# A feed-forward block on one core: down projection in rounded halves over three engines, selection keys in PSUM, transposes between products

## The reference, cut to what matters

```python
inter = xf @ c1_w.T @ c2_w.T                       # rank 16, 1792 columns
blk = inter.reshape(B * T, n_blocks, SPARSITY)     # 56 blocks of 32
idx = jnp.argmax(blk, axis=-1) + jnp.arange(0, INTER, SPARSITY)
h = jax.nn.relu(jnp.einsum('bkm,bm->bk', w1[idx], xf))
out = jnp.einsum('bk,bkm->bm', h, w2t[idx])
```

## Time and profile before

| | us |
|---|---|
| median of 3 runs (lowest to highest) | 625.63 (625.03 to 625.82) |
| the profiled execution's own time | 625.32 |
| its span in the trace | 623.3 |

### The profile page before, as it was taken

One profiled execution on the slowest core, in us unless ns is written; L12 is line 12 of the kernel. 1 busy time (PEld: TensorE's weight loads), 2 busy tenths in 40 slices (PEclk: granted clock), 3 DMA queues, 4 the chain that ended last, 5 costly groups with the idle time before them and its releaser, 6 DMA issues.

```text
span 623.3 us, 10995 instructions
## 1 busy us (share of the span) xinstructions
PE 611.2 (98%) x3900; PEld 523.7 (84%) x3900; DVE 437.0 (70%) x882; ACT 332.6 (53%) x613; POOL 222.8 (36%) x181
## 2 busy tenths in 40 slices
PE   8999999999999999999999989999999999999997
PEld 8888888799898999899988989997979779787573
DVE  4533137678888888888886768799794774858773
ACT  2513115668676867677776635755544554447110
POOL 0000002269778877887786712224012021000000
PEclk9999999999999999999999999999999999999999
DMA  7500011878887788788778929485765767697500
GB/s 263 226 0 31 5 38 40 214 191 213 215 213 198 202 213 214 200 209 212 178 178 227 340 98 302 153 323 201 270 252 218 282 221 261 252 366 312 195 1 17
DMA packets 29693, 120.67 MB, mean 194 GB/s; under 512 B 7712, under 2 KB 8224, under 8 KB 22096
## 3 DMA queue, kind: packets, MB, share of 16 engines
q1 hardware_dynamic: 28912, 118.96, 61.1%
q10 hardware_dynamic: 576, 1.05, 0.6%
q0 software_dynamic: 160, 0.07, 0.1%
HBM read 86.30 MB, written 0.26 MB: 139 GB/s over the span
## 4 chain that ended last, share of the span: by engine, by line
PE 81%; POOL 6%; DVE 6%; issue 4%; ACT 3%; DVEq 0%; ACTq 0%; POOLq 0%
PE ps L1767 20%; PE ps L1466 10%; PE ps L1467 10%; PE ps L1468 10%; PE ps L1807 9%; PE ps L1567 4%; POOL pt_lo L542 3%; PE ps L1796 2%; PE ps L1643 2%; PE ps L1918 2%; DVE prob_far L1116 2%; PE ps L1510 2%; PE ps L1527 2%; POOL v_lo L542 2%; PE ps L1881 2%
## 5 line engine op out<-in xcount | busy, mean ns | idle before, releaser
L1767 PEld LDWEIGHTS ps<-norm_t,ring 128*128 128x128 f32 x1152 | 131.6, 192 | 4.9 <-issue 4.1
L1767 PE MATMUL ps<-norm_t,ring 128*128 128x128 f32 x1152 | 133.2, 276 | 0.0
L542 POOL TENSOR_TENSOR pt_lo<-far_t,pt_hi 128x512 fp32r<-128x512 f32 (+1 forms) x94 | 111.8, 1216 | 55.1 <-ACT pt_hi L658 54.6
L732 ACT ACTIVATE prob_far<-prob_far,neg_max 128x1024 f32<-128x1024 f32 (+2 forms) x96 | 85.5, 892 | 55.2 <-DVE neg_max L1120 55.2
L1116 DVE TENSOR_SCALAR_CACHE_REDUCE prob_far<-ps 128x256 f32<-128x256 f32 (+2 forms) x96 | 86.8, 906 | 31.9 <-PE ps L1468 31.5
L1297 DVE SCALAR_TENSOR_TENSOR acc<-raw,cw,acc 128x127 f32<-128x127 f32 (+2 forms) x240 | 77.0, 397 | 19.5 <-ACT acc L909 18.9
L1140 DVE STREAM_TRANSPOSE prob_far<-prob_far 128x2176 f32<-128x2176 f32 x30 | 73.1, 2436 | 0.8 <-ACT prob_far L732 0.2
L1466 PE MATMUL ps<-pt_hi,v_hi 128*128 128x256 f32 x208 | 61.2, 294 | 2.7 <-POOL pt_lo L542 2.3
L1466 PE MATMUL ps<-k_hi,q_hi 128*128 128x512 f32 (+2 forms) x160 | 61.4, 384 | 1.4 <-ACT v_all L658 0.7
L1468 PE MATMUL ps<-pt_lo,v_hi 128*128 128x256 f32 x208 | 58.8, 283 | 0.0
L1467 PE MATMUL ps<-pt_hi,v_lo 128*128 128x256 f32 x208 | 58.7, 282 | 0.0
(11 more groups left out here) (228 smaller groups left out, 1144.1 us busy)
## 6 DMA issues: line engine op xcount, KB each, us to landing
ring<-w_in_dram SPq DMA_DIRECT2D x36, 1024.0 KB, 4.9
far_t<-prob_far SPq DMA_DIRECT2D x240, 136.0 KB, 2.6
ring<-w_out_dram SPq DMA_DIRECT2D x16, 1024.0 KB, 4.8
ring<-wq_dram SPq DMA_DIRECT2D x16, 512.0 KB, 4.1
ring<-wo_dram SPq DMA_DIRECT2D x16, 512.0 KB, 3.6
w_sb<-w_dram SPq DMA_DIRECT2D x4, 896.0 KB, 9.1
ring<-ctx_t_dram SPq DMA_DIRECT2D x3, 1024.0 KB, 5.1
ring<-w_dram SPq DMA_DIRECT2D x3, 1024.0 KB, 8.8
```

The costliest lines, as they stand in the source:

```text
L542: sub = lambda dst, a, hi: pool.tensor_tensor(dst, a, hi, ALU.subtract)
L732: nc.scalar.activation(tile, tile, ACT.Exp, bias=neg_max[:, b, h:h + 1], accum_out=part_sum[:, b, h, i:i + 1]).then_inc(exp_ok, 1)
L1767: ins = mm(ps[:, bank, t * T:t * T + T], w[:, t, c, :], norm_t[:, c, :], start=(c == 0), stop=(c == NC - 1))
```

## The change

The down projection is done as three rounded products per tile. The work of splitting goes to three engines:
- ScalarE: `w2_high(c)` copies chunk c of `w2` from `ring` into the new `w2_hi` (rounded); chunk 0 ahead of the wait for the square root of L999, chunk 1 behind it, chunks 2 and 3 behind the copy `r1_st`. The copies out of PSUM now write `hsel_hi` in the rounded type.
- GpSimd: `ring_lo = ring - w2_hi`, in place, in pieces of 1024 columns (two, two, two and one), each chunk behind its copy.
- VectorE: `selected_low(i)` subtracts `hsel_hi` from the transposed quarter in PSUM. Number 0 comes behind the first step of quarter 2's selection, number 1 behind the fourth, 2 and 3 behind all of the selection.

The keys of the selection stay in PSUM bank i: the two equality and product steps write there, in place, only the last mask goes to SBUF (`key[i % 2]`). `key` and `hsel` are two buffers of 512 columns each in place of one of 1792. `turn_over(2)` now comes behind tile 5 of the down projection and `turn_over(3)` behind tile 9. `w2_hi` is laid over buffers of the state-space block, which are moved for it; the final sum is written into `normed` in place of `final`. The number of transfers and their sizes are the same.

```diff
@@ -246,13 +246,13 @@
                 bc = sbuf(st4, "bc", [P, 16, T])
                 gm = sbuf(st4, "gm", [P, GROUPS, T])
                 with ExitStack() as st5:
-                    key_flat = sbuf(st5, "key", [P, FF])
-                    hsel = sbuf(st5, "hsel", [P, FF])
-                    hsel_t = sbuf(st5, "hsel_t", [P, NFT, T])
+                    key = [sbuf(st5, f"key{b}", [P, BANK]) for b in range(2)]
+                    hsel = [sbuf(st5, f"hsel{b}", [P, BANK]) for b in range(2)]
+                    hsel_hi = sbuf(st5, "hsel_hi", [P, NFT, T], F32R)
+                    hsel_lo = sbuf(st5, "hsel_lo", [P, NFT, T], F32R)
                     rank = sbuf(st5, "rank", [P, BLK])
                     norm_hi = sbuf(st5, "norm_hi", [P, NC, T], F32R)
                     norm_lo = sbuf(st5, "norm_lo", [P, NC, T], F32R)
-                    final = sbuf(st5, "final", [P, DM])
                 raw = [sbuf(st4, f"raw{b}", [P, 4, T]) for b in range(2)]
                 acc = [sbuf(st4, f"acc{b}", [P, 4, T]) for b in range(2)]
                 xc = [sbuf(st4, "xc0", [P, TPG, T])]
@@ -260,20 +260,21 @@
                 decay = [sbuf(st4, "decay0", [P, HPG, T])]
                 xc.append(sbuf(st4, "xc1", [P, TPG, T]))
                 sg.append(sbuf(st4, "sg1", [P, TPG, T]))
+                with ExitStack() as same_place:
+                    w2_hi = sbuf(same_place, "w2_hi", [P, NFT * DM], F32R)
+                at_pair.append(sbuf(st4, "at_pair1", [P, HPG, HALF_T], F32R))
+                at_hi.append(sbuf(st4, "at_hi1", [P, HPG, HALF_T], F32R))
+                at_lo.append(sbuf(st4, "at_lo1", [P, HPG, HALF_T], F32R))
                 decay.append(sbuf(st4, "decay1", [P, HPG, T]))
                 xdt = sbuf(st4, "xdt", [P, HPG, 64])
                 yv = sbuf(st4, "yv", [P, TPG, T])
                 ysq = sbuf(st4, "ysq", [P, TPG, T])
                 sq_tok = sbuf(st4, "sq_tok", [P, 2, T])
                 ug = [sbuf(st4, f"ug{b}", [P, TPG, T]) for b in range(2)]
-                at_pair.append(sbuf(st4, "at_pair1", [P, HPG, HALF_T], F32R))
-                at_hi.append(sbuf(st4, "at_hi1", [P, HPG, HALF_T], F32R))
-                at_lo.append(sbuf(st4, "at_lo1", [P, HPG, HALF_T], F32R))
 
                 with ExitStack() as same_place:
                     w1_lo = sbuf(same_place, "w1_lo", [P, NC, FF], F32R)
                 w1_sb = sbuf(st4, "w1_sb", [P, NC, FF])
-            key = key_flat[:].rearrange("p (n j) -> p n j", j=BLK)
 
         last_wo_hi = k_hi[:, 0:2 * DM].rearrange("p (h n) -> p h n", h=2)
         last_wo_lo = k_lo[:, 0:2 * DM].rearrange("p (h n) -> p h n", h=2)
@@ -321,6 +322,7 @@
                                                sem("nl_ok"))
         ug_ok, var_s = sem("ug_ok"), sem("var_s")
         f_mask = sem("f_mask")
+        w2h_ok, w2l_ok, htl_ok = sem("w2h_ok"), sem("w2l_ok"), sem("htl_ok")
         pair_const, a_pair_in = sem("pair_const"), sem("a_pair_in")
         stored = sem("stored")
 
@@ -527,7 +529,7 @@
                 s, before = stream(FFN0 + c)
                 load(s, w2[c] if c < 3 else w2_tail[0], before)
             sp.wait_ge(final_ok, 1)
-            sp.dma_start(out, final[:]).then_inc(stored, 16)
+            sp.dma_start(out, normed[:]).then_inc(stored, 16)
             sp.wait_ge(stored, 16)
 
 
@@ -651,6 +653,15 @@
                     sub(c2_st[64:64 + RANK, :], c2_sb[64:64 + RANK, :],
                         c2_st[64:64 + RANK, :].bitcast(F32)).then_inc(c2l_ok, 1)
                     pool.wait_ge(c2l_ok, 1)
+
+            for c in range(4):
+                slot, cols = stream(FFN0 + c)[0], min(SLOT, NFT * DM - c * SLOT)
+                pool.wait_ge(w2h_ok, c + 1)
+                for at in range(0, cols, SLOT // 2):
+                    part = slice(at, at + SLOT // 2)
+                    i = sub(ring_lo[slot][:, part], ring[slot][:, part],
+                            w2_hi[:, c * SLOT + at:c * SLOT + at + SLOT // 2].bitcast(F32))
+                i.then_inc(w2l_ok, 1)
 
 
         @block.scalar
@@ -995,8 +1006,19 @@
             mamba_step(6, 0, True)
 
             squares(GROUPS - 1)
+            def w2_high(c):
+
+
+                slot, before = stream(FFN0 + c)
+                cols = min(SLOT, NFT * DM - c * SLOT)
+                act.wait_ge(landed[slot], 16 * (before + 1))
+                act.wait_ge(*((seg_ps, 2 * GROUPS), (y_ps, GROUPS), (y_ps, GROUPS), (ug_ok, 2 * GROUPS))[c])
+                copy(w2_hi[:, c * SLOT:c * SLOT + cols], ring[slot][:, 0:cols]).then_inc(w2h_ok, 1)
+
+            w2_high(0)
             act.wait_ge(var_s, 4)
             nc.scalar.activation(rstd[:, 1:2], rstd[:, 0:1], ACT.Sqrt).then_inc(var_s, 1)
+            w2_high(1)
 
 
             norm_sqrt(2)
@@ -1004,10 +1026,12 @@
             copy(norm_hi[:], ps[:, 7, :].rearrange("p (c t) -> p c t", c=NC)).then_inc(nh_ok, 1)
             act.wait_ge(r1_ps, 1)
             copy(r1_st[:], ps[0:STACK, 6, 0:T]).then_inc(r1h_ok, 1)
+            w2_high(2)
+            w2_high(3)
             for i in range(4):
                 w = min(4, NFT - 4 * i)
                 act.wait_ge(ht_ps, i + 1)
-                copy(hsel_t[:, 4 * i:4 * i + w, :],
+                copy(hsel_hi[:, 4 * i:4 * i + w, :],
                      ps[:, i, 0:w * T].rearrange("p (c t) -> p c t", t=T)).then_inc(ht_ok, 1)
 
 
@@ -1425,30 +1449,45 @@
             sub(r1_st[32:32 + RANK, :], ps[32:32 + RANK, 6, 0:T],
                 r1_st[32:32 + RANK, :].bitcast(F32)).then_inc(r1l_ok, 1)
             dve.wait_ge(pool_const, 8)
+            def selected_low(i):
+
+                w = min(4, NFT - 4 * i)
+                dve.wait_ge(ht_ok, i + 1)
+                sub(hsel_lo[:, 4 * i:4 * i + w, :], ps[:, i, 0:w * T].rearrange("p (c t) -> p c t", t=T),
+                    hsel_hi[:, 4 * i:4 * i + w, :].bitcast(F32)).then_inc(htl_ok, 1)
+
             for i in range(4):
                 lo, hi = i * BANK, min(i * BANK + BANK, FF)
                 n0, n = lo // BLK, (hi - lo) // BLK
-                blocks = ps[:, i, 0:hi - lo].rearrange("p (n j) -> p n j", j=BLK)
-                k, top, first = key[:, n0:n0 + n, :], bmax[:, n0:n0 + n], kmax[:, n0:n0 + n]
+                k = ps[:, i, 0:hi - lo].rearrange("p (n j) -> p n j", j=BLK)
+                top, first = bmax[:, n0:n0 + n], kmax[:, n0:n0 + n]
                 dve.wait_ge(inter_ps, i + 1)
-                nc.vector.tensor_reduce(top, blocks, AX_X, ALU.max).then_inc(f_mask, 1)
+                nc.vector.tensor_reduce(top, k, AX_X, ALU.max).then_inc(f_mask, 1)
+                if i == 2:
+                    selected_low(0)
                 dve.wait_ge(f_mask, 5 * i + 1)
-                nc.vector.tensor_tensor(k, blocks, top.unsqueeze(2).to_broadcast([P, n, BLK]),
+                nc.vector.tensor_tensor(k, k, top.unsqueeze(2).to_broadcast([P, n, BLK]),
                                         ALU.is_equal).then_inc(f_mask, 1)
                 dve.wait_ge(f_mask, 5 * i + 2)
                 nc.vector.tensor_tensor(k, k, rank[:].unsqueeze(1).to_broadcast([P, n, BLK]),
                                         ALU.mult).then_inc(f_mask, 1)
                 dve.wait_ge(f_mask, 5 * i + 3)
                 nc.vector.tensor_reduce(first, k, AX_X, ALU.max).then_inc(f_mask, 1)
+                if i == 2:
+                    selected_low(1)
                 dve.wait_ge(f_mask, 5 * i + 4)
-                nc.vector.tensor_tensor(k, k, first.unsqueeze(2).to_broadcast([P, n, BLK]),
+                chosen = key[i % 2][:, 0:hi - lo]
+                nc.vector.tensor_tensor(chosen.rearrange("p (n j) -> p n j", j=BLK), k,
+                                        first.unsqueeze(2).to_broadcast([P, n, BLK]),
                                         ALU.is_equal).then_inc(f_mask, 1)
                 dve.wait_ge(f_mask, 5 * i + 5)
                 dve.wait_ge(h_ps, i + 1)
-                nc.vector.scalar_tensor_tensor(hsel[:, lo:hi], ps[:, 4 + i, 0:hi - lo], 0.0, key_flat[:, lo:hi],
+                nc.vector.scalar_tensor_tensor(hsel[i % 2][:, 0:hi - lo], ps[:, 4 + i, 0:hi - lo], 0.0, chosen,
                                                ALU.max, ALU.mult).then_inc(hsel_ok, 1)
+            selected_low(2)
+            selected_low(3)
             dve.wait_ge(ffn_ps, 1)
-            nc.vector.tensor_tensor(final[:], res[:], ps[:, 4, :], ALU.add).then_inc(final_ok, 1)
+            nc.vector.tensor_tensor(normed[:], res[:], ps[:, 4, :], ALU.add).then_inc(final_ok, 1)
 
 
         @block.tensor
@@ -1888,7 +1927,8 @@
 
                 pe.wait_ge(hsel_ok, i + 1)
                 for t in range(4 * i, min(4 * i + 4, NFT)):
-                    ins = nc.tensor.transpose(ps[:, i, (t % 4) * T:(t % 4 + 1) * T], hsel[:, t * T:t * T + T], ident[:])
+                    ins = nc.tensor.transpose(ps[:, i, (t % 4) * T:(t % 4 + 1) * T],
+                                              hsel[i % 2][:, (t % 4) * T:(t % 4 + 1) * T], ident[:])
                 ins.then_inc(ht_ps, 1)
 
```

(26 more changed lines are left out.)

## The result

| | before | after |
|---|---|---|
| median of 5 runs, us (lowest to highest) | 625.03 (624.72 to 625.82) | 627.54 (626.85 to 628.72) |
| ratio to before, 95% interval | | 1.0039 (1.0028 to 1.0049) |
| profiled execution: its time; its span | 625.32; 623.3 | 627.54; 625.8 |

The kernel is 2.5 us slower, where 1.3 was forecast; the time lies inside the range of 624.2 to 627.9.

The account below looks back on a forecast made before the run. TensorE was taken to bound the kernel, except VectorE's chain at the layer norm. From the profiled 625.32, stalls add 2.62 and the tail gives 1.3: 626.6, or 626.9 us against the median; range 624.2 to 627.9.

Parts of the forecast that it names:

- The products: Down projection on TensorE: 42 rounded passes of 0.2325 us replace 28 of 0.430, 2.28 us less if TensorE never waits.
- Who feeds them: Down projection: TensorE waits for VectorE's low half only ahead of tile 8, 0.95 us; the tail gains 1.3 us.
- Keys in PSUM: VectorE's selection steps: PSUM operands taken to cost 0, at most 0.06 us more for each of 16 steps.
- ScalarE's copies: The w2_high copies, 1.92 us per full chunk, fit into ScalarE's idle time and cost nothing.
- The first stall: w1_split(3), ahead of the layer norm, waits for GpSimd's piece 2: +0.52 us on the chain, 1.1 us being slack.
- The second stall: normed in the layer norm waits for GpSimd's piece 4: 2.1 us of the +2.6 on the chain.
- Rival B: Layer norm: normed isn't held by GpSimd, only the 0.52 us remains, 624.9 us; chance 0.24.
- the last rival, F: TensorE's clock falls after the longer pause at the layer norm: some 3 us more, 630; chance 0.05.
- A: Likeliest case: GpSimd holds both w1_split(3) and normed around the layer norm, 626.9 us; chance 0.52.
- rival D: Selection steps that write PSUM are dearer, +0.06 us on 16 steps: 627.9 us, or 625.9 without norm stall; 0.09 beside A.

Follow-up runs that it names:

- e6: e1 with selected_low(2) moved ahead of the last two steps of quarter 3's selection: 623.04 us against 625.28 before the change.
- e7: e1 with the selection's keys written to SBUF again instead of PSUM: 629.36 us against 625.28 before the change.
- e1: The change with all of GpSimd's pieces started only behind the copy norm_hi, after the layer norm: 623.48 us against 625.17 before the change.
- e2: The change with only the first chunk's two GpSimd pieces early, the other five behind norm_hi: 623.97 us against 625.17 before the change.
- e3: The change with the layer norm's sum written to PSUM and normed reading it there: 625.35 us against 625.17 before; once more, 624.97 against 625.14.
- e5: The change with GpSimd's pieces halved to 512 columns, 14 instead of 7: 624.41 us against 625.28 before the change.
- e4: The change with 22 instead of 12 warming products on TensorE: 626.07 us against 625.17 before the change.
- e12: The change with the edits of e2 and e3 and 16 instead of 12 warming products: 624.29 us against 625.40 before the change.

## Why the prediction was right, and where it was off

- **The products**: 0.2325 us per pass was forecast; chain and timeline of after show 0.23. In e6, where no stall is left in the norm, selection to store takes 21.76 us against 23.66, 1.90 less, with 0.35 of delay left at tile 8 (its chain has 0.11 us of issue there and 0.47 us for a pass instead of 0.23). 1.90 + 0.35 = 2.25, against 2.28.
- **Who feeds them**: right by place and size. One wait, ahead of tile 8, 0.83 us against 0.95, none elsewhere. The restart adds a little (starts of 616.76 and 617.98 lie 1.22 apart instead of 0.23, and the next one 0.31), so the tail gave 1.10 and not 1.3.
- **Keys in PSUM**: I took 0 and it was 0.01: 0.70 where a step writes PSUM. The bound of 0.06 a step wasn't needed. That they cost nothing is the small part of it; e7 shows what they save, of which my prediction said nothing, as it costed only their price.
- **ScalarE's copies**: 1.90 us for a full chunk, under cover, as forecast; the square root still waits for VectorE (1.4 us).
- **The first stall**: +0.52 forecast, +0.48 measured, 0.45 by e1 and e2. The mechanism, read from the earlier trace rows, held within 0.05 us: `w1_split(3)` took 3.65 us against the 3.70 of the sum.
- **The second stall**: +2.1 forecast, +1.98 measured on the step itself. Piece 4 was 0.09 us ahead of `normed`, where I had 0.05. Rival B was refuted on the point that it hung on; e3 and e5 confirm the reason.
- **What failed** is the last rival, F, by its weight: "A small chance", with 0.05. It came with A, in all five executions. TensorE's pause of 2.83 us was followed by 1.45 us of loss (e4: 1.47). Its price was off as well, "some 3 us": the lower level held from about 597.3 to 600.7, not for all of the products behind the pause. Without the clock the tail would have grown by 1.32 us, as in e4, and the forecast of +1.3 was made for that. I had the pause in the working (593.0 to 596.0) and knew of no row of before with a pause that long at the full clock. A thing that no row covers should have been in the sum with its bounds, 0 and 3 us, like the writes to PSUM, not put aside.
- **What was luck**: the likeliest case was put at 626.9, the measured loss is nearly twice the 1.3 forecast, and 627.54 lies in the range only because the range went up to 627.9 for rival D, dearer steps that write PSUM. D didn't happen (0.70 us a step); the room that was left for it took in the clock. The 0.3 us outside the span, which the forecast didn't have, helped a little.

## What to carry to other kernels

An engine that idles is not free for work if its operands lie in SBUF: in these runs a GpSimd subtraction held up every VectorE step that was issued beside it and drew on SBUF twice (two inputs there, or one input there at two elements at a time), for the whole rest of its length, and whether `normed` lost 2 us was decided by less than 0.1 us. Before giving GpSimd something, list those steps of VectorE on the critical chain, and put GpSimd's start behind the last of them (one semaphore here: 4 us), or give those steps an operand in PSUM. And a wait that leaves TensorE without work should be priced twice, once for itself and once for the clock behind it; here no execution showed it after pauses of up to 0.85 us, about half of them after 1.1, and all after 2.8, and products that only keep TensorE busy took the loss away (e4, e12).

## What the runs showed of the hardware

- A VectorE cast of 32 numbers, SBUF to SBUF, took 0.17 us alone and 0.95 to 1.24 us beside GpSimd's pieces (e3, e5): the length of the held step doesn't matter.
- A held VectorE step ended a fixed time behind the piece that held it: 0.28 us for `normed` (the change, e5), 0.55 for two-input steps of 512 columns (e7), 1.9 for `w1_split(3)` with 1792 (the change: 588.85 to 590.73).
- The granted clock of TensorE fell from 2.4 to 1.2 GHz for a part of the time after a pause of 2.83 us that was followed by stages with further gaps of 0.69 us, and again in e7 after one of 2.78. After pauses of up to 0.85 us no execution shows it, after 0.95 one of 10, after 1.1 us 15 of 33, after 2.8 us all 9.
- Writing a selection step into PSUM in place, source and result in the same bank, took 0.70 us for 512 columns against 0.69 from or to SBUF.
